# Loads of the second layer's expert blocks released by the gating of eight blocks before instead of by its landed results

## The chip, the cores and the metric

One core of a Trainium2 chip runs the whole kernel. The metric is the device time of one execution in microseconds (us), the median over several.

## What is computed

A two-layer vision transformer on 128 images. Each image is cut into 64 patches; with a class token it has 65 tokens of 128 numbers, 8320 tokens in all. Layer 0 has an attention and a mixture of 32 experts; layer 1 has a decay-weighted mixing within each image and a mixture of 16 experts with 512 hidden units, top 2 per token. The change touches this last part. Cut to what matters, the reference says:

```python
logits = xt @ router_w.T + router_b
probs = jax.nn.softmax(logits, axis=-1)
topk_p, topk_i = lax.top_k(probs, TOP_K)
gates = ...  # the two chosen probabilities of each token, 0 elsewhere
def expert_step(acc, packed):
    w1e, b1e, w2e, b2e, ge = packed
    h = jax.nn.gelu(xt @ w1e.T + b1e, approximate=False)
    y = h @ w2e.T + b2e
    return (acc + y * ge[:, None], None)
```

and the result is added to the layer's input, `h = h + ...`.

## The kernel before

**Dispatch.** Tokens go through in groups: 13 groups (`MG`) of 5 tiles of 128 tokens in the second layer. For each token and each of its two experts, GpSimd sends a row of 132 numbers to a list of that expert in DRAM, with an indirect DMA of 128 rows each (`send`, line 2554; ten sends for a group). A row holds the normalized token, and behind it where its result belongs (`PLACE`), its gate, and two numbers from which the token's own value is restored (`SPREAD`, `MEAN`). Tables made from the counts say which expert and which stretch of its list each block takes (`tb.entry`).

**Blocks.** The second layer's experts are worked off in 81 blocks (`L1.blocks`). 64 are full, with 256 list rows (two tiles); 17 are half, with 128 rows (one tile), every other block from 25 to 57. Block i uses buffers `u = i % 8`: `wblk` for an expert's weights (578 KB) and `xblk` for its rows (132 KB if full), both loaded by `load_part` from SyncE (lines 614 and 616), and `yblk` for the results. For each block:

- TensorE transposes the rows (`t1`, line 987, two blocks ahead), makes the first product (`t2`, line 1010 for full blocks, 1013 for half ones, one block ahead) and the second one (`t3`, line 1032).
- ScalarE copies the first weights to a rounded form (`high`) and applies GELU (line 1408).
- VectorE splits rows and weights for TensorE (`xT`, lines 2147 to 2152). Then `gated` restores the tokens' own values (line 2158), waits until `yblk` of eight blocks before has landed (line 2167), adds a bias to TensorE's second product (line 2173), and multiplies by the gate and adds (line 2184). The last of these instructions raises `y_ready`.
- GpSimd waits for `y_ready` and sends the results to their places in DRAM with one indirect DMA a tile (`send_results`, line 2582), which raise `y_out[u]` when they have landed. It reads the places out of `xblk`. In the first layer it reads them out of a buffer of their own, `place`, which VectorE fills (line 2169).

Because GpSimd reads `xblk` late, the loads of block i in the second layer wait at line 610 until the results of block i-8 have landed. In the first layer they wait for `y_ready`. Each engine does its work in the order in which it is written; SyncE's order is `sp_blocks`: the first eight blocks' loads, 17 writes of padding rows to the lists (`pads`), then one load a block. Before block 24 (`L1.early`) it waits until every list row and padding row has landed (`dispatched`).

**The last lists.** When the blocks begin, the ten sends of each of the last two groups are not all out: GpSimd sends 4 of group 11 ahead of the blocks and the other 16 one by one, one after each block's results.

**Finished groups.** A group whose results are complete is read back (`load_end`, line 725, 640 KB, four buffers), its two results a token are added by VectorE (`total`, line 2491) and stored by ScalarE's queue (line 1547). Groups 0 to 6 go among the blocks: SyncE reads them behind loads 65, 67, 69, 71, 73, 75 and 77 (`end_at`), VectorE adds them three blocks before those positions; their landings are implied by the waits of the loads. Groups 7 to 12 come after the blocks, with an explicit wait for landings (`landed`).

Of the kernel before, what the change touches and what calls it, by code (L numbers as in the profile page):

```python
# [23 lines left out]
U32 = mybir.dt.uint32  # L24
# [14 lines left out]
TILES = 5  # L39
ROWS = GT // TILES  # L40
HALF = GT // 2
TOP = 2
# [17 lines left out]
MG = TOKENS // (TILES * WIDE)  # L60
# [208 lines left out]
def build(nc, a, out):  # L269
    ctx = ExitStack()  # L270
    with ctx:
# [330 lines left out]
        def load_part(eng, l, u, j, part):  # L602

            k = K[l.name]
            i = l.unroll * j + u
            at, q, first, n = l.loads[i][part]
            entry = eng.value_load(tb.entry[0:1, at:at + 1], min_val=0, max_val=l.E * l.step - 1)  # L607
            e, r = entry // l.step, entry % l.step
            if l is L1:
                eng.wait_ge(k.y_out[u], k.y0[u] + 16 * l.packets(i))  # L610
            elif i >= l.unroll:
                eng.wait_ge(k.y_ready, i - l.unroll + 1)
            weights = third[u] if part == 2 else wblk_of[l.name][u][:, part * l.W:(part + 1) * l.W]
            eng.dma_start(weights, a[f"w_{l.name}"][bass.ds(e * 128, 128), :]).then_inc(k.blk_in[u], 16)  # L614
            tiles = max(n // 128, 1)
            eng.dma_start(xblk[u][first:first + n // tiles, q:q + tiles, :].rearrange("p q w -> p (q w)"),  # L616
                          lists[l.name][bass.ds(r, n), :].rearrange("(p q) w -> p (q w)", q=tiles))\
                .then_inc(k.blk_in[u], 16)
# [34 lines left out]
        @block.sync  # L653
        def _(sp):
            def load_patches(g, h, j):
                for c in range(CHUNKS):
                    sp.wait_ge(chunk_used[h][c], j)
                    sp.dma_start(xin[h][c][:, :, :].rearrange("p k n -> p (k n)"),
                                 a["x_main"][bass.ds(g * CHUNKS + c, 1), :, :].rearrange("o p n -> (o p) n"))\
                        .then_inc(chunk_in[h][c], 16)  # L660
                    if c == CHUNKS - 1:
                        sp.dma_start(xrest[h][:, :], a["x_rest"][bass.ds(g, 1), :, :]
                                     .rearrange("o p n -> (o p) n")).then_inc(chunk_in[h][c], 16)
            pairs(sp, load_patches)
            def load_rows(g):
                h, j = g % 2, g // 2
                if j > 0:
                    sp.wait_ge(m_free[h], j)
                sp_group_in(sp, "L0", g, h, yin, m_in[h])

            def load_distance(g):
                if g > 0:
                    sp.wait_ge(m_spread, g)
                sp.dma_start(m_dist[:, :, :].rearrange("p t c -> p (t c)"), a["distance"][g]).then_inc(dist_in, 16)

            def load_difference(g):
                h = g % 2
                if g > 1:
                    sp.wait_ge(delta_ps, 2 * (g - 1))
                sp.dma_start(m_delta[h][:, :, :].rearrange("p t c -> p (t c)"), a["difference"][g])\  # L680
                    .then_inc(delta_in[h], 16)

            def mid_class(g):

                done = (g + 1) * TILES * WIDE - 1
                return L0.class_of(done // (TILES * ROWS))

            def landed(l, enough):

                for b in range(max(0, enough - NB), enough):  # L690
                    sp.wait_ge(K[l.name].y_out[b % NB], K[l.name].y0[b % NB] + 16 * (l.packets(b) + l.tiles_of(b)))

            def rows_landed(g):
                landed(L0, L0.enough(mid_class(g)))
                load_rows(g)

            def early(g):
                if g + 2 >= 0:
                    yield 5, load_difference, g + 2
                yield 6, rows_landed, g + 3  # L700
                if g + 2 >= 0:
                    yield 7, load_distance, g + 2

            among = Among(early)
            for h in range(2):
                for c in range(CHUNKS):
                    sp.wait_ge(chunk_used[h][c], GROUPS // 2)
            sp_blocks(sp, L0, among)
            among.left()
            rows_landed(LAST + 4)  # L710
            load_difference(LAST + 3)
            load_distance(LAST + 3)
            load_difference(LAST + 4)
            rows_landed(LAST + 5)
            for g in range(LAST + 4, MG):
                if g + 2 < MG:
                    rows_landed(g + 2)
                if g + 1 < MG:
                    load_difference(g + 1)
                load_distance(g)  # L720

            def load_end(g, u, j):
                if j > 0:
                    sp.wait_ge(e_ready, g - NZ + 1)
                sp.dma_start(end_y[u].rearrange("p t k d -> p (t k d)"),
                             results["L1"].rearrange("(g p t k) d -> g p (t k d)", g=MG, p=WIDE, t=TILES)[g, :, :])\
                    .then_inc(e_in[u], 16)

            for u in range(NB):
                sp.wait_ge(K["L1"].y_out[u], K["L1"].y0[u])  # L730
            sp_blocks(sp, L1, ends(load_end, 0))

            def load_left(g, u, j):
                landed(L1, L1.enough(L1.class_of(g)))
                load_end(g, u, j)
            ends_left(load_left)


        @block.tensor
# [818 lines left out]
        def _(dve):  # L1558
# [563 lines left out]
            def expert_blocks(l, behind=None):  # L2122
# [39 lines left out]
                def gated(u, j):  # L2162
                    i = U * j + u
                    p2 = u % 2
                    restore(u, j)
                    Q = l.tiles_of(i)
                    dve.wait_ge(k.y_out[u], k.y0[u] + 16 * l.packets(i))
                    if l is L0:
                        dve.tensor_copy(place[:, u, :], xblk[u][:, :, PLACE].bitcast(U32))
                    dve.wait_ge(k.y_ps, k.i0 + i + 1)  # L2170
                    y = ps[:, banks(l, i)[2], 0:Q * D].rearrange("p (q d) -> p q d", q=Q)
                    if l.FC > 1:
                        dve.tensor_tensor(yblk[u][:, 0:Q, :], y,  # L2173
                                          wblk[u][:, None, l.W - D:l.W].to_broadcast([128, Q, D]), ALU.add)\
                            .then_inc(y_biased, 1)
                        dve.wait_ge(y_biased, i + 1)
                        y = yblk[u][:, :, :]
                    dve.wait_ge(restored, k.i0 + i + 1)
                    of = [(0, 128, q, q) for q in range(Q)]
                    if l.mixed[i]:  # L2180
                        of = [(0, 128, 0, 0), (0, 64, 1, 1), (64, 128, 1, 2)]
                        y = ps[:, banks(l, i)[2], 0:3 * D].rearrange("p (q d) -> p q d", q=3)
                    for first, end, q, product in of:
                        ins = dve.scalar_tensor_tensor(yblk[u][first:end, q, :], y[first:end, product, :],  # L2184
                                                       xblk[u][first:end, q, GATE:GATE + 1],
                                                       xblk[u][first:end, q, 0:D], ALU.mult, ALU.add)
                    ins.then_inc(k.y_ready, 1)
# [311 lines left out]
        def _(pool):  # L2499
# [75 lines left out]
            def expert_blocks(l, behind=None):  # L2575
                k = K[l.name]
                def send_results(u, j):
                    pool.wait_ge(k.y_ready, k.i0 + l.unroll * j + u + 1)
                    past(pool, pool_passed)
                    for q in range(l.tiles_of(l.unroll * j + u)):  # L2580
                        where = place[:, u, q:q + 1] if l is L0 else xblk[u][:, q, PLACE:PLACE + 1].bitcast(U32)
                        pool.indirect_dma_start(  # L2582
                            out=results[l.name], out_offset=bass.IndirectOffsetOnAxis(ap=where, axis=0),
                            in_=yblk[u][:, q, :], in_offset=None, bounds_check=last, oob_is_err=False)\
                            .then_inc(k.y_out[u], 16)
                    if behind:
                        behind(l.unroll * j + u)

                if l is L0:
                    rounds(pool, l, send_results)  # L2590
                    return
                of = list(itertools.product((MG - 2, MG - 1), range(TILES * TOP)))[4:]
                for i in range(l.blocks):
                    send_results(i % l.unroll, i // l.unroll)
                    for g, n in of[i:i + 1]:
# [10 lines left out]

            for g in range(LAST + 1, MG - 2):
                send(L1, g, g % 2)
            send(L1, MG - 2, MG % 2, 0, 4)
            expert_blocks(L1)  # L2610


# [64 lines left out]
```

## Time and profile before

| | |
|---|---|
| median of 3 runs | 1091.51 us (1088.7 to 1091.65) |
| the profiled execution | 1087.39 us, span 1085.7 us |
| TensorE busy | 914.5 us (84%) |
| VectorE busy | 847.8 us (78%) |
| GpSimd busy | 678.9 us (63%) |
| ScalarE busy | 503.9 us (46%) |
| DMA | 246.57 MB, mean 227 GB/s |

The span runs from the first to the last instruction of one profiled execution; its time is beside it, and the runs of the median were made apart from it. Shares are over the whole span, in which stages of different kinds follow each other: patches and first attention to about 430 us, first experts to about 660, second mixing to about 800, second experts to about 1066, and the last groups.

### The profile page before, as it was taken

The page shows a single profiled execution, that of the slowest core. Times are in us where ns is not written, and L with a number is a line of the kernel's source. Part 1 is how long each engine was busy: PE and PEld are TensorE (multiplying, and loading weights), DVE is VectorE, ACT ScalarE, POOL GpSimd, SP SyncE. Part 2 cuts the span into 40 slices and gives each one's busy share as a digit, 9 for nine tenths or more (in the row PEclk, how much of TensorE's full clock was granted, in tenths as well). Part 3 has the DMA queues.
Part 4 walks back from the last instruction along what each step waited for, and adds up shares of the span by engine and source line. Part 5 has one row for each costly group of instructions (what it writes and reads, how often), then busy time and mean ns, then how long its engine had stood idle before and what let it go on. Part 6 is the DMA issues. An engine that isn't in the chain of part 4 may idle for free.

```text
span 1085.7 us, 21714 instructions
## 1 busy us (share of the span) xinstructions
PE 914.5 (84%) x6064; PEld 772.5 (71%) x6064; DVE 847.8 (78%) x3318; ACT 503.9 (46%) x1342; POOL 678.9 (63%) x622
## 2 busy tenths in 40 slices
PE   6999999999999987476776877778569999999992
PEld 2577666677777666475665766677469989999992
DVE  1488889898888998666677899888667877778983
ACT  1355555555555442211112554777435655556561
POOL 1016666666676645677677767777777775545553
PEclk9999999999999997578887988877769999999996
DMA  9956566655566304577779973865188688889986
GB/s 371 353 206 217 202 217 222 222 201 201 201 206 211 123 21 116 152 209 206 210 219 310 293 259 120 265 228 169 59 302 263 231 253 277 275 279 301 356 325 235
DMA packets 118664, 246.57 MB, mean 227 GB/s; under 512 B 20914, under 2 KB 85936, under 8 KB 112400
## 3 DMA queue, kind: packets, MB, share of 16 engines
q1 hardware_dynamic: 77440, 191.26, 52.7%
q0 software_dynamic: 18592, 34.68, 9.4%
q10 hardware_dynamic: 22512, 19.25, 5.8%
q8 instruction: 48, 0.79, 0.3%
q14 instruction: 72, 0.59, 0.2%
HBM read 201.68 MB, written 45.43 MB: 228 GB/s over the span
## 4 chain that ended last, share of the span: by engine, by line
PE 39%; DVE 20%; issue 11%; DMA 11%; ACT 7%; SPq 6%; POOL 4%; ACTq 1%; DVEq 0%; POOLq 0%
PE ps L1032 6%; DMA xin<-lists_L 4%; PE ps L1010 4%; PE ps L762 4%; DMA results_L<-xin 3%; PE ps L1130 3%; POOL results_L L2582 3%; PE ps L829 3%; PE ps L1133 3%; PE ps L813 2%; SPq L614 2%; SPq L616 2%; PE ps L786 2%; SPq L607 2%; ACT x_hi L1211 2%
## 5 line engine op out<-in xcount | busy, mean ns | idle before, releaser
L2554 POOL DMA_INDIRECT lists_L<-rows,slots x230 | 263.4, 1145 | 153.3 <-issue 151.7
L2582 POOL DMA_INDIRECT results_L<-xin x145 | 146.2, 1008 | 96.3 <-DVE xin L2184 64.0
L2582 POOL DMA_INDIRECT results_L<-xin,place x146 | 144.1, 987 | 58.8 <-issue 39.3
L762 PE MATMUL ps<-xin,w_emb 128*128 128x512 f32 x292 | 137.7, 608 | 9.9 <-DMA w_emb<-in_w_main 8.3
L1032 PE MATMUL ps<-xin,QK 128*128 128x128 f32 x838 | 115.5, 289 | 2.6 <-DVE xin L2184 2.5
L1032 PEld LDWEIGHTS ps<-xin,QK 128*128 128x128 f32 x838 | 107.8, 204 | 4.5 <-issue 4.1
L2563 POOL TENSOR_TENSOR x_lo<-xin,x_hi 128x2048 fp32r<-128x2048 f32 x13 | 60.1, 4623 | 63.5 <-ACT x_hi L1219 63.1
L987 PE MATMUL ps<-ident,xin 128*128 128x128 f32 x291 | 66.3, 309 | 38.2 <-DMA xin<-lists_L 35.1
L1408 ACT ACTIVATE QK<-ps,xin 128x256 f32<-128x256 f32 x164 | 64.3, 475 | 70.9 <-PE ps L1010 70.9
L762 PEld LDWEIGHTS ps<-xin,w_emb 128*128 128x128 f32 x292 | 52.8, 194 | 58.9 <-issue 48.1
L2158 DVE TENSOR_SCALAR xin<-xin 128x128 f32<-128x128 f32 x291 | 92.7, 367 | 0.6
L1032 PE MATMUL ps<-xin,UH 128*128 128x128 f32 x648 | 89.2, 283 | 2.7 <-DVE xin L2184 2.7
L1238 ACT ACTIVATE h0T<-ps 128x256 f32<-128x256 f32 x73 | 27.9, 383 | 134.1 <-PE ps L987 90.2
L1032 PEld LDWEIGHTS ps<-xin,UH 128*128 128x128 f32 x648 | 81.7, 198 | 3.9 <-issue 3.8
L1010 PE MATMUL ps<-x_hi,x_lo 128*128 128x256 f32 x256 | 78.6, 307 | 0.7 <-DVE x_lo L2152 0.7
L1005 PE MATMUL ps<-h0T,xin 128*128 128x128 f32 (+1 forms) x326 | 60.3, 323 | 17.6 <-ACT h0T L1238 6.4
L1010 PE MATMUL ps<-x_lo,x_hi 128*128 128x256 f32 x256 | 73.1, 286 | 0.0
L1010 PE MATMUL ps<-x_hi 128*128 128x256 f32 x256 | 73.1, 286 | 0.0
L987 PEld LDWEIGHTS ps<-ident,xin 128*128 128x128 f32 x291 | 38.6, 157 | 47.4 <-DMA xin<-lists_L 43.0
L1408 ACT ACTIVATE UH<-ps,xin 128x256 f32<-128x256 f32 (+1 forms) x160 | 55.6, 430 | 32.8 <-PE ps L1010 29.1
L2173 DVE TENSOR_TENSOR xin<-ps,xin 128x256 f32<-128x256 f32 x81 | 32.2, 397 | 49.2 <-PE ps L1032 49.2
L1005 PEld LDWEIGHTS ps<-h0T,xin 128*128 128x128 f32 x326 | 54.0, 238 | 20.4 <-issue 11.6
(408 smaller groups left out, 2436.4 us busy)
## 6 DMA issues: line engine op xcount, KB each, us to landing
xin<-in_x_main SPq DMA_DIRECT2D x48, 1536.0 KB, 6.7
xin<-in_w_L SPq DMA_DIRECT2D x81, 578.0 KB
xin<-in_w_L SPq DMA_DIRECT2D x98, 128.0 KB
xin<-lists_L SPq DMA_DIRECT2D x64, 132.0 KB
xin<-in_w_L ACTq DMA_DIRECT2D x65, 128.0 KB
x_hi<-results_L SPq DMA_DIRECT2D x13, 640.0 KB, 6.3
xin<-in_difference SPq DMA_DIRECT2D x13, 640.0 KB
xin<-in_distance SPq DMA_DIRECT2D x13, 640.0 KB, 6.6
```

The costliest lines, as they stand in the source:

```text
L762: mm = pe.matmul(psE[h], w_emb[:, k, :], xin[h][c][:, n, :], start=(k == 0), stop=False, skip_group_check=True)
L829: mm = pe.matmul(pair[2][:, c:c + SEQ], V[h][:, i, :], Pr[h][:, i, :], start=True, stop=True)
L987: mm = pe.transpose(ps[:, banks(l, i)[0], q * 128:(q + 1) * 128], xblk[b][:, q, 0:D], ident[:, :])
L1005: mm = pe.matmul(bank_h(i, f)[:, of_part], w1, xTb[p2][:, of_part], start=True, stop=True)
L1010: mm = pe.matmul(bank_h(i, f)[:, 0:n_in], w[p2][:, cols_f], x[p2][:, 0:n_in], start=(n2 == 0), stop=(n2 == 2), skip_group_check=True)
L1032: mm = pe.matmul(o, hTb[p2][:, f, rows_in], w2[:, f * D:(f + 1) * D], start=(f == 0), stop=(f == l.FC - 1))
L1130: mm = pe.matmul(o, matrix[:, t, 0:WIDE], m_norm[g % 2][:, t, :], start=True, stop=alone, skip_group_check=True)
L1408: ins = act.activation(hTb[p2][:, f, 0:n_in], ps[:, 2 + 2 * p2 + f // 2, f % 2 * l.block:f % 2 * l.block + n_in], ACT.Gelu, bias=b1)
L2158: ins = dve.tensor_scalar(xblk[u][:, q, 0:D], xblk[u][:, q, 0:D], xblk[u][:, q, SPREAD:SPREAD + 1], xblk[u][:, q, MEAN:MEAN + 1], ALU.mult ...
L2554: pool.indirect_dma_start(out=lists[l.name], out_offset=bass.IndirectOffsetOnAxis(ap=slots_of(l, g, h)[:, t, k:k + 1], axis=0), in_=buf[:, ...
L2563: pool.tensor_tensor(x_lo0[:, :, :].rearrange("p k n -> p (k n)"), xin[h][0][:, 0:KS, :].rearrange("p k n -> p (k n)"), x_hi0[:, :, :].rea ...
L2582: pool.indirect_dma_start(out=results[l.name], out_offset=bass.IndirectOffsetOnAxis(ap=where, axis=0), in_=yblk[u][:, q, :], in_offset=Non ...
```

## The change

The loads of the second layer wait for `y_ready` of the block eight before, as those of the first do. So that `xblk` is free by then, VectorE copies the places to `place` in the second layer too, and GpSimd reads them there. Since a load no longer implies a landing, each read of a finished group among the blocks now waits for the landings it needs (`end_landed`), the same call as after the blocks. GpSimd sends 6 of group 11's lists ahead of the blocks instead of 4, and 14 among them instead of 16.

```diff
@@ load_part @@
-            if l is L1:
-                eng.wait_ge(k.y_out[u], k.y0[u] + 16 * l.packets(i))
-            elif i >= l.unroll:
-                eng.wait_ge(k.y_ready, i - l.unroll + 1)
+            if i >= l.unroll:
+                eng.wait_ge(k.y_ready, k.i0 + i - l.unroll + 1)
@@ block.sync @@
-            sp_blocks(sp, L1, ends(load_end, 0))
-
-            def load_left(g, u, j):
+            def end_landed(g, u, j):
                 landed(L1, L1.enough(L1.class_of(g)))
                 load_end(g, u, j)
-            ends_left(load_left)
+            sp_blocks(sp, L1, ends(end_landed, 0))
+            ends_left(end_landed)
@@ vector, gated @@
                     dve.wait_ge(k.y_out[u], k.y0[u] + 16 * l.packets(i))
-                    if l is L0:
-                        dve.tensor_copy(place[:, u, :], xblk[u][:, :, PLACE].bitcast(U32))
+                    dve.tensor_copy(place[:, u, :], xblk[u][:, :, PLACE].bitcast(U32))
@@ gpsimd @@
-                        where = place[:, u, q:q + 1] if l is L0 else xblk[u][:, q, PLACE:PLACE + 1].bitcast(U32)
                         pool.indirect_dma_start(
-                            out=results[l.name], out_offset=bass.IndirectOffsetOnAxis(ap=where, axis=0),
+                            out=results[l.name], out_offset=bass.IndirectOffsetOnAxis(ap=place[:, u, q:q + 1], axis=0),
...
-                of = list(itertools.product((MG - 2, MG - 1), range(TILES * TOP)))[4:]
+                of = list(itertools.product((MG - 2, MG - 1), range(TILES * TOP)))[6:]
...
-            send(L1, MG - 2, MG % 2, 0, 4)
+            send(L1, MG - 2, MG % 2, 0, 6)
```

## Rows read from the trace of the kernel before

**Rows 1.** Windows over the block stage and its last part, with their columns' heading.
```profile
core 0: us, PE busy (x) PEld busy (x) DVE busy (x) ACT busy (x) POOL busy (x), PEclk, DMA share, GB/s
806.00:1066.00 260.00, 252.59 (x2181) 249.20 (x2179) 203.88 (x577) 150.37 (x381) 159.47 (x160) 1.00 0.86 285
1020.00:1050.00 30.00, 29.25 (x256) 29.06 (x255) 26.95 (x72) 18.12 (x44) 16.90 (x17) 1.00 1.01 377
```

**Rows 2.** Waits from 806 to 1066 us: total, times, longest, in us.
```profile
SPq L614 <- DMA results_L<-xin: 92.7, 49, 4.6
...
DVE xin L2173 <- PE ps L1032: 48.8, 70, 1.7
...
PE ps L987 <- DMA xin<-lists_L: 7.0, 11, 1.9
```

**Rows 3.** Chain that ended last, in order of time: start, us, what.
```profile
868.04 4.41 DMA results_L<-xin
...
873.21 5.14 DMA xin<-lists_L
```

**Rows 4.** Timeline of TensorE: transposes of blocks 8, 22, 46 and 72.
```profile
825.89 0.44 PE L987 MATMUL ps<-ident,xin 128*128 128x128 f32 x2 [0.77 <-DMA xin<-lists_L]
...
878.40 0.44 PE L987 MATMUL ps<-ident,xin 128*128 128x128 f32 x2 [1.91 <-DMA xin<-lists_L]
...
948.38 0.44 PE L987 MATMUL ps<-ident,xin 128*128 128x128 f32 x2 [1.03 <-DMA xin<-lists_L]
...
1029.62 0.44 PE L987 MATMUL ps<-ident,xin 128*128 128x128 f32 x2 [0.75 <-DMA xin<-lists_L]
```

**Rows 5.** Timeline of SyncE: pad rows, then the weight loads of these blocks.
```profile
806.48 13.47 SPq L591 DMA_DIRECT2D lists_L<-padrows  x16
820.91 0.35 SPq L614 DMA_DIRECT2D xin<-in_w_L  x1
...
872.65 0.33 SPq L614 DMA_DIRECT2D xin<-in_w_L  x1
...
942.01 0.33 SPq L614 DMA_DIRECT2D xin<-in_w_L  x1
...
1020.74 0.33 SPq L614 DMA_DIRECT2D xin<-in_w_L  x1
```

**Rows 6.** Timeline of VectorE: gating of blocks 14, 38 and 64.
```profile
857.60 0.61 DVE L2184 SCALAR_TENSOR_TENSOR xin<-xin 128x128 f32<-128x128 f32 x2
...
934.31 0.62 DVE L2184 SCALAR_TENSOR_TENSOR xin<-xin 128x128 f32<-128x128 f32 x2
...
1012.25 0.61 DVE L2184 SCALAR_TENSOR_TENSOR xin<-xin 128x128 f32<-128x128 f32 x2
```

**Rows 7.** VectorE: copies' durations (min/median/max) and group mean; then its timeline.
```profile
L2169 DVE COPY place<-xin x73: 148/164/428, 455.7 to 661.2; 128x2 uint32<-128x2 uint32 x73
...
L2169 DVE COPY place<-xin 128x2 uint32<-128x2 uint32 x73 | 14.6, 199 | 0.0
...
1020.39 0.42 DVE L2147 CAST x_hi<-ps 128x256 fp32r<-128x256 f32 x1
...
1025.54 0.42 DVE L2173 TENSOR_TENSOR xin<-ps,xin 128x256 f32<-128x256 f32 x1 [0.47 <-PE ps L1032]
...
1026.53 0.82 DVE L2491 TENSOR_TENSOR xin<-x_hi 128x640 f32<-128x640 f32 x1
1027.27 0.42 DVE L2147 CAST x_hi<-ps 128x256 fp32r<-128x256 f32 x1
```

**Rows 8.** Timeline of GpSimd: last send ahead, first results, lists after blocks 13, 15.
```profile
806.49 0.97 POOL L2554 DMA_INDIRECT lists_L<-values,slots  x1 [0.30 <-issue]
809.94 0.99 POOL L2582 DMA_INDIRECT results_L<-xin  x1 [2.49 <-DVE xin L2184]
...
865.46 0.97 POOL L2554 DMA_INDIRECT lists_L<-rows,slots  x1 [0.30 <-issue]
...
873.26 0.97 POOL L2554 DMA_INDIRECT lists_L<-rows,slots  x1 [0.30 <-issue]
```

## The prediction

> **What bounds the kernel now.** I read the page first, to find the stage that the diff touches: the second layer's expert blocks, 81 of them, run from about 806 to 1066 us of the span. Then the table of windows for that stage. TensorE is busy for 252.6 of its 260 us, at a granted clock of 1.00 (its 2.4 GHz level); VectorE for 203.9, GpSimd for 159.5, the DMA engines for 0.86 of the time [rows 1]. So the stage is TensorE's. Whatever the change does to the loads, it can't give more than TensorE's idle 7.4 us there.
>
> Next the waits of the stage. Nearly all of TensorE's idle time has one reason: 7.0 us in 11 pieces, each before the transposes that open a block (line 987), each ended by a load that arrives [rows 2]. The SyncE queue, which issues these loads, waits 92.7 us in 49 pieces at line 614 for landed results [rows 2]. The chain of waits joins the two. A result leaves GpSimd at 868.04 and lands 4.41 us later; that frees block 22's load, which takes 5.14 us; and TensorE starts the block at 878.40, 1.91 us late [rows 3, 4]. What the diff removes is therefore on the path, but only where the load comes late. Elsewhere it is hidden.
>
> **Waits removed.** Today load i needs block i-8's results in DRAM; afterwards it needs only VectorE's last gating instruction of block i-8 (line 2184). For three of the late blocks I compare the time at which TensorE wanted the block (its start less the idle time) with both releases.
> - Block 22: wanted at 878.40 - 1.91 = 876.5, issued at 872.65, so 3.8 us of lead where 5.75 were needed. Gating of block 14 ended at 857.60 + 0.61 = 858.2: lead 18.3 us [rows 4 to 6].
> - Block 46: wanted at 947.35, issued at 942.01, lead 5.3, needed 6.4. Gating of block 38 ended at 934.93: lead 12.4 [rows 4 to 6].
> - Block 72: wanted at 1028.87, issued at 1020.74, lead 8.1, needed 8.9. Gating of block 64 ended at 1012.86: lead 16.0 [rows 4 to 6].
>
> The slowest of these loads took 8.9 us, and the shortest new lead is 12.4. So these waits go entirely. The 0.77 us before block 8 stay: its load left at 820.91 because the queue had been issuing the 16 pad rows since 806.48 (13.47 us), which the diff leaves where they are [rows 4, 5]. Gain: 7.01 - 0.77 = 6.24 us. What is late next? Nothing on TensorE's side: in these 260 us its only releaser by name is the load.
>
> **The copy of the places.** VectorE now does the copy of line 2169 for these 81 blocks too. The first layer runs it 73 times at a mean of 199 ns [rows 7], so 81 x 0.2 = 16 us of VectorE. It stands between restoring the rows and the wait for TensorE's product. Over the stage VectorE waits there for TensorE 48.8 us in 70 pieces [rows 2]: that hides it. The tightest stretch is where the additions of finished groups (line 2491) run among full blocks: two blocks and one addition take from 1020.39 to 1027.27, 6.88 us, of which VectorE idles 0.47 [rows 7]. Two copies take 0.40 of that. TensorE's period there is the same 6.88, so the copy still fits, by 0.07 us a pair, and costs nothing. If it did not fit it would cost at most 2 x 0.428 - 0.47 = 0.39 us a pair with the longest copy seen [rows 7], and 0 with the mean one; over the 7 additions 0 to 2.7 us. I take 0, as the mean is the nearer row, and keep 2.7 for the range.
>
> **Two lists in front.** GpSimd idles 2.49 us before the first results at 809.94. A list send follows every 1.27 us (0.97 and 0.30 of issue), so two more after 806.49 end at 810.3, and the first results leave 0.36 us later [rows 8]. Nothing on TensorE's path waits for them any more. In return the last list leaves after block 13's results, where a list starts at 865.46 today, instead of after block 15's, at 873.26 [rows 8]. SyncE waits for all lists before load 24. With the 4.41 us that a scatter took to land [rows 3], they are down at 865.8 + 4.4 = 870.2 instead of 877.7. That is 7.5 us earlier, while the blocks have by then moved up by less than the whole gain, 6.2 us. With 877.7 no idle piece fell on block 24, so with 870.2 none will. Cost 0; GpSimd would have to fall at least 1.3 us behind today's pace before anything could show.
>
> **The reads of finished groups.** Their loads (line 725) now wait for landings themselves. Only the first, at block 65, can hold the queue: it waits for block 57's results, which is what load 65 waits for today, so it is no later than now. Load 66, behind it, may lose a landing's 4.4 us of a lead like block 72's 16. Cost 0. VectorE's own wait before it reuses a result buffer (line 2167) is for results eight blocks old, 8 x 3.44 = 27.5 us in full blocks; block 14's, in the worst of GpSimd's backlog, were down at 872.45, 14.2 us after their gating at 858.2 [rows 3, 6]. Cost 0. The end (results of the last block, four reads of finished groups, addition, store) only moves up.
>
> **The sum.** The profiled execution took 1087.39 us (span 1085.7). 1087.39 - 6.24 + 0 = 1081.2. The three timed runs lie higher, with a median of 1091.51, so 4.12 above the execution whose rows I used. The same gain from that median gives 1091.51 - 6.24 = 1085.3, my forecast.
>
> **Rivals.**
> - *Loads that take longer (0.14).* The engines are busy for 0.86 of the stage and 1.01 in 1020 to 1050, at 377 GB/s [rows 1]. Loads issued 7 to 14 us earlier lie beside each other in the queues and each may take longer. For it: the slowest of the three rows took 8.9 us in that very stretch. Against it: the bytes are the same, and a load must take over 12 us before TensorE notices. With half of the waits left: 1091.5 - 3.1 = 1088.4.
> - *The queue is held all the same (0.08).* SyncE goes in order, so if the lists before load 24 or the landing at block 65 hold it, the loads behind are as late as today. This is the change that doesn't do what it says. It takes GpSimd to fall behind by 1.3 us or more, or a landing at block 65 far over 4.4 us; the send rows show an even pace of 1.27 us. Time: 1090 to 1091.5.
> - *VectorE becomes the bound (0.05), the slower side.* If the copy waits for GpSimd's sends, it isn't 0.2 us long. The first layer's longest is 0.428 against a shortest of 0.148 [rows 7]; a send lasts 0.97 [rows 8]. The addition takes 1027.27 - 1026.53 = 0.74 us of VectorE's time, so a full block without it takes (6.88 - 0.47 - 0.74)/2 = 2.83 of a period of 3.44 and has room for 0.61 [rows 7]; beside an addition there is room for 0.235. Copies of 0.75 us would cost 14 x (0.75 - 0.235) = 7.2 us in the last third and 50 x (0.75 - 0.61) = 7.0 over the other full blocks, 14.2 in all, less the 6.24 gained: 1091.5 + 8.0 = 1099.5. From about 0.63 us a copy the change loses. Of 73 copies none reaches that. The Trainium skill has a rule that leads there: SBUF — State Buffer, "Who interferes with whom", says that VectorE copies in a two-port mode and GpSimd share a port pair under an exclusive lock, and that the later one blocks fully. By that rule alone a copy could last a whole send more. The rows of the first layer, where the sends run as well, agree at most for a part of one.
>
> The rest, 0.03, is unforeseen. The forecast has 0.70.
>
> **How the numbers follow.** Under the forecast alone I expect 1083 to 1087.5: the gain of 6.24, up to 2.7 back for the copy, and about as much to the other side for an execution with more late loads than the profiled one. The range of 1081.5 to 1089.5 adds the rival of longer loads and runs that differ by 3 us among themselves. It leaves out the held queue, the slow copies and the tails. A measurement of this kernel tells about 0.3%, 3.3 us, from no change. Faster by more: nearly all of the forecast (0.69) and a third of the longer loads (0.05), so 0.74. Within: the rest of those and the held queue, 0.21. Slower: 0.05.
>
> **What would show it.** In the profile after: TensorE idle for loads in the stage about 0.8 us, at block 8; line 614's wait at SyncE released by line 2184 instead of a DMA; the copy in the stage at about 0.2 us x81, VectorE's busy time there up by 16 us and its idle time down by as much; the first results about 0.4 us later; the chain of waits through the blocks all TensorE. The prediction is wrong if pieces of idle time before line 987 stay in the second half of the stage, if TensorE waits at lines 1010 or 1032 for VectorE, or if its busy time in the stage rises.

## The result, and the profile after

The changed kernel takes 1083.08 us, the median of 6 runs (1082.49 to 1085.35); the kernel before, in 6 runs beside them, 1090.11 (1087.42 to 1091.93). The ratio is 0.9943, with a 95% interval of 0.9926 to 0.996: 6.2 us faster by the ratio, 7.0 by the two medians. The forecast was 1085.3 in a range of 1081.5 to 1089.5, and faster had 0.74. The sign, the place and the range were right. The sum was not right in its parts: one term was too small, one was missing, and the two partly cancel.

The profiled execution of the changed kernel has a span of 1081.3 us, against 1085.7. Windows over its block stage and the last part, columns as in [rows 1]:

```profile
806.00:1066.00 260.00, 252.68 (x2198) 252.24 (x2197) 211.69 (x664) 150.68 (x386) 164.44 (x164) 0.99 0.87 291
1020.00:1050.00 30.00, 30.00 (x264) 30.00 (x263) 28.16 (x84) 17.86 (x44) 17.38 (x18) 1.00 0.78 287
```

The first window now holds all of the stage from 806 us on and some of what follows it, because the stage ends at 1059 us. So its sum for TensorE is about that of [rows 1], and that says nothing. The second window lies inside the stage in both: TensorE went from 29.25 to 30.00 of 30 us.

Waits from 806 to 1066 us (total, times, longest): SyncE for its loads, VectorE for the second product, and TensorE for a load, first in the queue of weight loads (PEld) and then in that of matmuls (PE).

```profile
SPq L612 <- DVE xin L2180: 66.4, 55, 1.9
...
DVE xin L2169 <- PE ps L1029: 33.3, 54, 1.6
...
PEld ps L984 <- DMA xin<-lists_L: 0.8, 1, 0.8
...
PE ps L984 <- DMA xin<-lists_L: 0.6, 1, 0.6
```

Line 612 is the old 614, and line 2180 the gating of the old 2184. SyncE still waits at line 612 for a long time, but for the gating and no longer for a landing, and that wait is idle time of an engine off the path. Of TensorE's 11 pieces [rows 2] one is left, before block 8 (old line 987 is 984). The reason is where it was, 16 pad rows ahead of load 8 in SyncE's queue; SyncE's timeline and TensorE's:

```profile
809.01 14.12 SPq L591 DMA_DIRECT2D lists_L<-padrows  x16
824.24 0.35 SPq L612 DMA_DIRECT2D xin<-in_w_L  x1
```

```profile
829.37 0.44 PE L984 MATMUL ps<-ident,xin 128*128 128x128 f32 x2 [0.63 <-DMA xin<-lists_L]
```

The end of the stage on GpSimd, the results of blocks 78, 79 and 80 (two sends each). This is what the forecast did not have:

```profile
1056.07 0.98 POOL L2577 DMA_INDIRECT results_L<-xin,place  x1 [1.16 <-DVE xin L2180]
1057.35 0.98 POOL L2577 DMA_INDIRECT results_L<-xin,place  x1 [0.30 <-issue]
1061.71 1.04 POOL L2577 DMA_INDIRECT results_L<-xin,place  x1 [3.38 <-issue]
...
1065.61 0.98 POOL L2577 DMA_INDIRECT results_L<-xin,place  x1 [0.30 <-issue]
```

Gating of block 79 ended at 1058.5, yet its first send starts at 1061.71, after 3.38 us in which GpSimd waits for nothing that the profile shows. In the kernel before no such gap stands there; its first send of block 79 follows the gating:

```profile
1065.96 0.98 POOL L2582 DMA_INDIRECT results_L<-xin  x1 [0.96 <-DVE xin L2184]
1067.24 1.44 POOL L2582 DMA_INDIRECT results_L<-xin  x1 [0.30 <-DVE xin L2184]
...
1070.27 0.98 POOL L2582 DMA_INDIRECT results_L<-xin  x1 [0.30 <-issue]
```

The chain that ended last runs through TensorE alone from block 8 to the end of the blocks, then through that send and the read behind it:

```profile
824.83 4.50 DMA xin<-lists_L
...
1055.60 3.72 PE ps L1029 x32
...
1065.61 2.26 DMA results_L<-xin,place
...
1069.85 7.87 DMA w_emb<-results_L
```

**The balance of the two profiles.** Take as the stage the time from block 2's transposes, the first inside it, to the end of the last matmul. Block 2's rows, before and after:

```profile
803.36 0.63 PE L987 MATMUL ps<-ident,xin 128*128 128x128 f32 x2
```

```profile
806.82 0.63 PE L984 MATMUL ps<-ident,xin 128*128 128x128 f32 x2
```

- The stage took 1065.9 - 803.4 = 262.5 us before and 1059.3 - 806.8 = 252.5 after: 10.0 less (10.06 in hundredths).
- It began 3.46 us later (806.82 - 803.36). The two lists can't have made that: in all five profiles with six lists in front the two added ones are sent 3 us or more after block 2's start (here at 809.95 and 811.22). In the profiles of this study block 2 starts between 800.0 and 806.0 with four lists in front (eight kernels) and between 803.6 and 807.8 with six (five kernels). I take it as spread between executions; what makes it stays open.
- The tail, from the last matmul to the end of the span, took 1085.7 - 1065.9 = 19.8 us before and 1081.3 - 1059.3 = 22.0 after: 2.2 more.

-10.06 + 3.46 + 2.20 = -4.40, the difference of the spans.

### The profile page after: what moved, and what is told of

The parts are those of the page before. It is cut to its first block, busy times and chain, and to the rows that moved or that the text cites. A ratio compares the mean times of both kernels' runs of the same rounds, so it can differ in the third digit from the quotient of the medians.

```text
span 1081.3 us, 21742 instructions
## 1 busy us (share of the span) xinstructions
PE 911.6 (84%) x6064; PEld 772.7 (71%) x6064; DVE 852.0 (79%) x3399; ACT 501.8 (46%) x1342; POOL 677.5 (63%) x622
## 4 chain that ended last, share of the span: by engine, by line
PE 46%; DVE 17%; issue 11%; SPq 8%; POOL 6%; ACT 5%; DMA 5%; ACTq 1%; DVEq 0%; POOLq 0%
PE ps L1029 12%; PE ps L1007 8%; POOL lists_L L2550 5%; PE ps L759 4%; PE ps L826 3%; PE ps L810 2%; SPq L614 2%; SPq L612 2%; SPq L607 2%; ACT x_hi L1208 2%; PE ps L984 2%; PE ps L1127 2%; PE ps L798 2%; PE ps L752 2%; PE ps L1130 1%
## 5 line engine op out<-in xcount | busy, mean ns | idle before, releaser
L2577 POOL DMA_INDIRECT results_L<-xin,place x291 | 289.6, 995 | 152.5 <-DVE xin L2180 79.5
L1002 PEld LDWEIGHTS ps<-h0T,xin 128*128 128x128 f32 x326 | 53.4, 236 | 21.4 <-issue 10.7
L1235 ACT ACTIVATE atok<-ps 104x640 f32<-104x640 f32 x16 | 11.3, 705 | 104.0 <-PE ps L776 104.0
```

Source lines behind the costliest of these rows:

```text
L1002: mm = pe.matmul(bank_h(i, f)[:, of_part], w1, xTb[p2][:, of_part], start=True, stop=True)
L1235: return act.activation(dst, src, ACT.Copy)
L2577: pool.indirect_dma_start(out=results[l.name], out_offset=bass.IndirectOffsetOnAxis(ap=place[:, u, q:q + 1], axis=0), in_=yblk[u][:, q, :] ...
```

## The experiments

Below, "stage", "tail" and "idle" (TensorE's, for loads, by the matmul rows) are meant as above. Ratios are to the kernel before, on the same chip.

**The changed kernel again (e1)**, with no edit, as the yardstick for the runs beside it.

> The changed kernel once more, as the base of the others. My theory: the whole gain is TensorE's waits for late loads in the second layer's blocks, so 0.992 to 0.996 of the kernel before (5 to 8 us less), with the stage about 10 us shorter by its first and last matmuls and TensorE idle for loads under 1 us. Rival (part of the difference came from where this one execution happened to stand before and after the stage): another ratio, 0.997 or more, with the same stage.

Measured: 1083.08 us, ratio 0.9946 (0.9926 to 0.9967). Stage 252.6, tail 21.9, and the same 3.38 us before block 79's results. So the gap belongs to the kernel, not to one execution.

**Only four lists in front (e2).** The change without its last part.

```diff
-                of = list(itertools.product((MG - 2, MG - 1), range(TILES * TOP)))[6:]
+                of = list(itertools.product((MG - 2, MG - 1), range(TILES * TOP)))[4:]
...
-            send(L1, MG - 2, MG % 2, 0, 6)
+            send(L1, MG - 2, MG % 2, 0, 4)
```

> The changed kernel with 4 lists in front instead of 6. My theory: the lists are off TensorE's path, so the same as the changed kernel within 1 us; the last list leaves GpSimd some 8 us later (about 878 instead of 870 us of the span) and SyncE's wait before load 24 grows from 5.3 to about 13 us, with the lead of load 24 still above 4 us. Rival: the lists in front carry part of the gain by keeping SyncE's wait before load 24 short; then TensorE idles before blocks 24 to 28 and 2 us or more of the gain go.

Measured: 1078.85 us, 0.991 (0.9893 to 0.9926), 4.2 us below e1, which ran beside it. Stage 252.8 as before, idle 0.7 in two pieces, tail 20.1. The results of block 79 leave on time:

```profile
1058.33 0.98 POOL L2577 DMA_INDIRECT results_L<-xin,place  x1 [0.96 <-DVE xin L2180]
```

So the lists in front seem to cost time instead of nothing. The tail shows 1.8 of the 4.2 us. Block 2 starts 2.2 us earlier than in e1 (805.56 against 807.81), ahead of the two added sends in e1 (811.37 and 812.65), so that part isn't theirs. The intervals of the two ratios meet at 0.9926, so the size of the difference is less sure than the gap itself.

**Only the copy (e3).** The kernel before, with the copy and GpSimd's reads out of `place` in both layers, and its loads still waiting for landings.

```diff
-                    if l is L0:
-                        dve.tensor_copy(place[:, u, :], xblk[u][:, :, PLACE].bitcast(U32))
+                    dve.tensor_copy(place[:, u, :], xblk[u][:, :, PLACE].bitcast(U32))
...
```

> The kernel before with the places copied by VectorE and read from their own buffer in both layers; loads still wait for landed results. My theory: the copy hides behind VectorE's waits for TensorE, so the same as before within 1.5 us. Rival (the copy costs): it delays the gating, and with it the results and the loads that wait for them, by 0.2 us a block where VectorE has no room, 1 to 3 us slower.

Measured: 1088.6 us, 1.0008 (0.9994 to 1.0023). The stage is 260.7 us, with 6.3 us of idle in nine pieces. The copy costs nothing that shows.

**Only the lists (e4).** The kernel before with six lists in front.

```diff
-            send(L1, MG - 2, MG % 2, 0, 4)
+            send(L1, MG - 2, MG % 2, 0, 6)
```

> The kernel before with 6 lists in front instead of 4 and nothing else. My theory: the loads up to 22 depend on results that have the same 14 lists ahead of them as before, so block 22's wait of 1.9 us stays; at most 1 us faster from later loads. Rival (GpSimd's backlog is the true cause and two sends less relieve it): 2 to 3 us faster, block 22's wait gone.

Measured: 1090.57 us, 1.0009 (0.9988 to 1.003). The stage is 262.6 us, so no gain; the gap stands before block 79's results here too, and the tail is 22.6. The tail is 2.8 us longer than in the kernel before; by the ratio the whole kernel is 1.0 us slower, and the interval would allow 2.8.

```profile
1070.05 1.04 POOL L2582 DMA_INDIRECT results_L<-xin  x1 [3.38 <-issue]
```

e3 and e4 together leave the gain to the one part that remains: what releases the loads. e2 has that part without the added lists and has the whole gain.

**How late may a load be (e5, e6, e9)?** On the version with four lists, the loads of the second layer wait for a block one, two or three later.

```diff
-                eng.wait_ge(k.y_ready, k.i0 + i - l.unroll + 1)
+                eng.wait_ge(k.y_ready, k.i0 + i - l.unroll + 1 + (1 if l is L1 else 0))
```

(2 and 3 in e6 and e9.)

> The changed kernel with 4 lists in front, and its second layer's loads released one block later (gating of block i-7). The lead of a load shrinks by one block, 2 to 3.4 us: for block 46 from 11.8 to about 9. My theory (a load needs 4 to 9 us, all earlier release is spare): the same as the run with the 4 lists, within 1 us, and TensorE idle for loads under 1.5 us. Rival (earlier is better without limit, because the DMA engines are then fed evenly): 2 to 4 us of the gain go.

Measured: 1080.45 us, 0.993 (0.9904 to 0.9955), with one wait of 1.74 us, at block 24.

> The same with the loads released two blocks later (gating of block i-6): lead of block 46 about 6.4 us, of full blocks about 9. My theory: now the slow loads come late again in the stretch of half blocks, where a load took 6.4 us and more in the kernel before; TensorE idles 1 to 5 us for loads, so 1 to 6 us slower than with the 4 lists. Rival (loads take 5 us once nothing else holds them): no change.

Measured: 1079.65 us, 0.9927 (0.99 to 0.9953), with one wait of 1.61 us, at block 8. Nothing in the rest of the stage, though the loads have 3.4 us less again in full blocks (8.8 us of lead, after 12.2 in e5). Load 46 on SyncE, and its block's transposes on TensorE, which follow 6.3 us later without a wait:

```profile
935.74 0.33 SPq L612 DMA_DIRECT2D xin<-in_w_L  x1
...
942.00 0.38 PE L984 MATMUL ps<-ident,xin 128*128 128x128 f32 x2
```

> The changed kernel with 4 lists in front and the second layer's loads released three blocks later (gating of block i-5): lead about 4 us in the half blocks, 5.5 in full ones, which is where the kernel before had it (3.8 to 8.1). My theory, after two blocks later cost nothing: between 4 and 6 us of lead it turns, so TensorE idles again before many blocks, 5 to 20 us, and most or all of the gain is gone (ratio to before 0.998 to 1.01). Rival (the waits of the kernel before came from something other than short leads, such as traffic of the results): few waits, ratio under 0.995.

Measured: 1107.86 us, 1.0175 (1.0142 to 1.0208). One block more, and about 27 us are lost (0.0248 of 1089 us by the two ratios): the stage is 278.6 us, TensorE waits 18 times for loads in it, 17 of them up to 1066 us, and load 46 leaves 4.7 us ahead of its transposes (949.37 and 954.08).

```profile
PE ps L984 <- DMA xin<-lists_L: 20.1, 17, 2.9
```

My reading, which no run separates, is that it feeds itself: a late load makes the block late, and the block's gating releases later loads late. The cliff lies between two and three blocks, and not at one figure of lead. In e9 blocks 11 to 17 wait for nothing with 5.4 us of lead, while blocks 68, 72 and 76, in the part where the finished groups are read, wait 2.93, 2.04 and 2.70 us, and their loads had left 8.2, 7.4 and 8.1 us before their transposes. In e6 those three had 8.8 us and no wait. So how much lead a load needs differs within the stage.

**Three copies (e7).** Two more copies a block into a buffer that nobody reads.

```diff
                     dve.tensor_copy(place[:, u, :], xblk[u][:, :, PLACE].bitcast(U32))
+                    if l is L1:
+                        for n_ in range(2):
+                            dve.tensor_copy(extra_places[:, u, n_, :], xblk[u][:, :, PLACE].bitcast(U32))
...
```

> The changed kernel with 4 lists in front and two more copies of the places a block, to a buffer that nobody reads: three copies, 0.6 us a block. By the room I worked out (0.235 us a block beside an addition, 0.61 elsewhere): 14 x (0.6 - 0.235) = 5 us slower than with the 4 lists, all of it from block 62 on, TensorE idle until VectorE there. Rival (VectorE works two blocks ahead of TensorE's need and carries a shortage over): under 1.5 us slower.

Measured: 1079.25 us, 0.9922 (0.9896 to 0.9949), against 0.991 in e2 and 0.9927 in e6: not slower by anything that the intervals show, where 5 us were expected. The stage is 254.1, of which 2.14 are block 8's wait. From 1000 to 1050 TensorE (first column) never idles, with VectorE (third) at 48.08 of 50:

```profile
1000.00:1050.00 50.00, 50.00 (x438) 50.00 (x437) 48.08 (x169) 29.93 (x72) 29.34 (x30) 1.00 0.81 304
```

VectorE's timeline says why three copies fit where I had room for one:

```profile
1007.37 0.17 DVE L2166 COPY place<-xin 128x2 uint32<-128x2 uint32 x1
1007.44 0.24 DVE L2169 COPY extra_places<-xin 128x2 uint32<-128x2 uint32 x2
...
1007.77 0.42 DVE L2173 TENSOR_TENSOR xin<-ps,xin 128x256 f32<-128x256 f32 x1
```

The second copy starts 0.07 us after the first, which is shown as 0.17 long. The rows overlap: a copy's row is the time that it takes, and the engine is free for the next one earlier.

**Pads out of the way of load 8 (e8).** On the version with four lists, the 16 pad rows go in four parts behind loads 10 to 13.

```diff
-            pads(sp, l, 0, PADS[l.name])
+            if l is L0:
+                pads(sp, l, 0, PADS[l.name])
...
+                i = l.unroll * j + u
+                if l is L1 and NB + 2 <= i < NB + 6:
+                    pads(sp, l, 4 * (i - NB - 2), 4 * (i - NB - 1))
```

> The changed kernel with 4 lists in front, and SyncE's pad rows sent in four parts behind the loads of blocks 10 to 13 instead of ahead of block 8's load, so that load 8 goes out as soon as block 0 is gated. My theory: the last 0.7 us of idle time before block 8 go and the loads behind have lead to spare, so 0.7 us faster than with the 4 lists. Rival (the pads hold loads 11 to 14 instead): no gain, an idle piece at block 12 to 15.

Measured: 1080.37 us, 0.9928 (0.9902 to 0.9954). Block 8's wait is gone, as it should be if the pads were its cause. But 2.11 us came back at block 24:

```profile
879.55 0.44 PE L988 MATMUL ps<-ident,xin 128*128 128x128 f32 x2 [2.11 <-DMA xin<-lists_L]
```

Load 24 left at 874.82, held until the last list had landed. In the changed kernel it leaves at 872.50 and has a lead of 11.9 us; in e2 it leaves at 878.83 with 4.6. So the lists in front do buy something, an earlier load 24. With four of them block 24 is at the edge once the blocks run faster: its load leaves 4.6 us ahead of its transposes in e2 and e6, without a wait; here and in e5 it leaves 4.7 and 5.2 us ahead, and of these 2.11 and 1.74 are the wait. With six lists and the new release none of the profiles has a wait there.

**The gap on GpSimd (e10, e11).** Where GpSimd stands still for over 1.5 us without a reason that the profile shows, counted in sends of results from the end: with four lists in front at the 52nd and 30th, with six at the 52nd, 34th and 4th (in e4 also at the 105th). One theory: it comes at fixed places of the instruction stream. e10 shifts the stream of the changed kernel by eight instructions on GpSimd.

```diff
             send(L1, MG - 2, MG % 2, 0, 6)
+            for _ in range(8):
+                past(pool, pool_passed)
```

> The changed kernel as it is, 6 lists in front, with eight semaphore increments more on GpSimd right before its blocks; they take under 0.5 us in all. In every profile with 6 lists GpSimd stands still for 3.4 us before the results of block 79, in none with 4. Theory A (the stall sits at fixed places of GpSimd's instruction stream): it moves some 8 instructions towards the start, to about block 77, where it is hidden, and the kernel gets 2.4 us faster than the changed one (ratio to before 0.992). Theory B (it belongs to the number of lists or to what is in flight then): it stays at block 79, and so does the time.

Measured: 1080.58 us, with the gap where it was and as long, so the theory of fixed places fell. The ratio is 0.9921 (0.9896 to 0.9946), 0.0022 below the changed kernel's own, and the intervals overlap widely. The profile shows the same tail (21.9) and gap, and a stage of 254.1 us, 1.6 longer, of which 1.4 are a longer wait at block 8 (2.06 us against 0.63). Nothing in it is faster, so I take the 0.0022 as spread.

```profile
1063.23 1.04 POOL L2577 DMA_INDIRECT results_L<-xin,place  x1 [3.38 <-issue]
```

e11 sends five lists ahead (`[5:]`, `send(L1, MG - 2, MG % 2, 0, 5)`).

> The changed kernel with 5 lists in front. Theory A: the order of two sends changes the stream before block 14 alone, and the stall sits somewhere else than with 4 or 6, by a place or two; if it is off block 79 the tail is 20 us instead of 22. Theory B (two more sends in front as such cause it): a stall of half the size, or one at block 79 as with 6.

Measured: 1079.63 us, 0.9909 (0.988 to 0.9938). The gap is at block 80's first send now, 1.63 us, and the tail is 21.4:

```profile
1058.39 1.44 POOL L2577 DMA_INDIRECT results_L<-xin,place  x1 [0.30 <-DVE xin L2180]
...
1061.46 0.98 POOL L2577 DMA_INDIRECT results_L<-xin,place  x1 [1.63 <-issue]
```

It was at the 4th send from the end with six lists, is at the 2nd with five, and with four there is none so late; the one before it is at the 34th, 32nd and 30th. So these two places move by one block for each list that goes in front, and the one at the 52nd stays. They depend on the order of the sends, and not on how many went before, which is the same at block 79 in all of them. What makes the gap is not settled. In its last 1.7 us (1060.00 to 1061.71 in the changed kernel) the DMA engines move nothing, so a transfer under way isn't what GpSimd waits for, and no packet of the instruction queues falls into it in any of the five profiles with six lists.

One rival is left. The send that ends the gap starts just before the end of two additions of VectorE, both operands of which lie in the buffers:

```profile
1060.34 0.82 DVE L2487 TENSOR_TENSOR xin<-x_hi 128x640 f32<-128x640 f32 x1
1061.08 0.82 DVE L2487 TENSOR_TENSOR xin<-w_emb 128x640 f32<-128x640 f32 x1
```

The send is 0.18 to 0.19 us ahead of that end in all five profiles with six lists (here 1061.71 and 1061.90), while e11's gap, beside which VectorE does nothing, is 1.63 us and not 3.38. So a part of the 3.38 us may be a wait for these additions. No run moves them, and they can't be the whole cause, since the same additions make no such gap in e2.

**Six lists and spread pads (e12),** with the eight increments of e10.

```diff
-            pads(sp, l, 0, PADS[l.name])
+            if l is L0:
+                pads(sp, l, 0, PADS[l.name])
...
             send(L1, MG - 2, MG % 2, 0, 6)
+            for _ in range(8):
+                past(pool, pool_passed)
```

> The changed kernel, 6 lists in front, with the pad rows spread behind loads 10 to 13 and the eight increments on GpSimd. If block 8's wait (0.7), block 24's (0 to 2 with 4 lists, none with 6) and the stall of the tail (2.4) are separate, all three are gone: TensorE idle under 0.3 us in the stage, tail 20 us, ratio to before 0.989 to 0.992, at least as fast as the run with the 4 lists. Rival (spread pads keep the lists' condition before load 24 late, or the stall stays): no faster than the changed kernel, 0.994.

Measured: 1079.83 us, 0.9902 (0.9876 to 0.9928). The stage is 252.4 us. One wait of 0.56 us is left, at block 14, and load 24 has its 11.9 us again; the gap of 3.38 us stays, and the tail is 22.7.

e2, e11 and e12 lie clearly below the kernel before (0.991, 0.9909, 0.9902) and by their medians below the changed one (0.9943 and 0.9946, and 0.9921 as e10). The lead over the changed kernel is 1 to 4 us; e12's interval, to 0.9928, overlaps the change's from 0.9926 by a hair, e11's by more. Which of the three is best these runs do not say. The plainest is e2: the change with the lists left as they were.

## Why the prediction was right, and where it wasn't

- **The waits removed: right, and mis-sized.** All pieces but block 8's are gone, SyncE's release is the gating, and e3 and e4 show that neither other part gives anything alone. The term "7.01 - 0.77 = 6.24 us" was too small: the stage is 10.0 us shorter. I had read the idle time from the matmul rows, whose ends are modelled and overlap what follows. The row of the weight loads in the kernel before, which I did not read, has more pieces and more time:

```profile
PEld ps L987 <- DMA xin<-lists_L: 10.3, 16, 2.1
```

  It went to 0.8, a gain of 9.5, near the 10.0 measured. The other runs bear this reading out. The stage less the waits of the weight loads in it is 251.3 to 252.4 us in thirteen of the fourteen profiles, e3 and e4 among them (254.0 in e9); less the waits of the matmul rows it goes from 251.7 to 255.5 in these thirteen, and the three with many waits stand at the top. My cap, "it can't give more than TensorE's idle 7.4 us", rested on the same rows and was wrong in the same way.
- **The copy: cost 0 was right, its working was not.** I priced it at 0.2 us of VectorE and left room for 0.07 us a pair. Its row is about that long,

```profile
L2165 DVE COPY place<-xin x81: 154/160/431, 810.6 to 1058.9; 128x2 uint32<-128x2 uint32 x81
```

  but it takes only about 0.07 us of the engine (e7), and VectorE's busy time from 806 to 1066 us rose by 7.8 us, not by 16. A pair of blocks with an addition is still 6.88 us, with 0.38 of idle time where there were 0.47 [rows 7]: 0.09 for two copies.

```profile
1012.96 0.42 DVE L2169 TENSOR_TENSOR xin<-ps,xin 128x256 f32<-128x256 f32 x1 [0.39 <-PE ps L1029]
...
1016.47 0.15 DVE L2165 COPY place<-xin 128x2 uint32<-128x2 uint32 x1
1016.54 0.41 DVE L2169 TENSOR_TENSOR xin<-ps,xin 128x256 f32<-128x256 f32 x1
...
1019.84 0.42 DVE L2169 TENSOR_TENSOR xin<-ps,xin 128x256 f32<-128x256 f32 x1 [0.38 <-PE ps L1029]
```

  So the rival of a bound VectorE was further off than its numbers said. The rule of the Trainium skill beside it (SBUF — State Buffer, "Who interferes with whom": the later one of a VectorE copy in a two-port mode and GpSimd blocks fully) would allow copies longer by a whole send. The longest of the 81, with a send under way for more than half of the stage, is 0.431 us against a send's 0.98, and the 162 extra ones of e7 reach 0.448. These rows do not show a block for a whole send, as the first layer's did not. They do show one for the end of a send, which I had overlooked. The longest copy, and the send under way beside it:

```profile
831.08 0.98 POOL L2577 DMA_INDIRECT results_L<-xin,place  x1 [0.30 <-issue]
...
831.63 0.43 DVE L2165 COPY place<-xin 128x2 uint32<-128x2 uint32 x1
```

  Both end at 832.06. The 17 copies that begin 0.55 to 0.68 us into a send take 0.25 to 0.43 us, and each ends within 0.04 us of its send; the 18 that begin earlier in a send take 0.15 to 0.16. So the trace agrees with the rule for the last 0.4 us or so of a send, and what a copy can lose by it is about 0.3 us.
- **Two lists in front: the step that failed.** I had "Cost 0", with the first results 0.36 us later. They are not later: they leave 0.8 us after their gating in both kernels. The cost is at the other end, where I wrote that the end "only moves up": the gap of 3.38 us before block 79's results, a tail 2.2 us longer, and by e1 and e2 4.2 us in the median. How much of that is the lists' is not shown: e10 and e12 send six ahead too, have the gap and a long tail, and their ratios are 0.9921 and 0.9902 against e2's 0.991. What the profiles show of the lists is the 1.8 to 2.8 us of the tail. I had looked at what the moved sends pass (the first results, load 24) and not at the sends behind them. What I said of load 24, that no idle piece would fall on it, came true; I did not see that with four lists one would (e5, e8).
- **The reads of finished groups: the cost of 0 was right, "only the first" was not.** The wait for a landing at block 65 makes load 66 late by 2.8 us (it leaves at 989.38, gating of block 58 ended at 986.54), and its lead of 13.1 us covers that. The read behind load 75 holds the queue as well: load 76 leaves at 1023.31, 2.4 us after the gating of block 68, with a lead of 13.5.

```profile
988.22 0.33 SPq L723 DMA_DIRECT2D w_emb<-results_L  x1
989.38 0.33 SPq L612 DMA_DIRECT2D xin<-in_w_L  x1
```

- **The other rivals.** Loads that take longer: not borne out for this change, since TensorE has no wait in the late part, and e6 runs there on 8.8 us of lead. I had said that a load must take over 12 us before TensorE notices; from block 12 on the shortest lead came out at 11.6, in the half blocks. The queue held all the same: three places, load 24 (4.0 us behind the gating of block 16, for the lists), load 66 (2.8) and load 76 (2.4), and no loss.
- **The sum.** I subtracted 6.24 from the median and got 1085.3. With the stage and the tail as the profiles show them it would have been 1091.5 - 10.0 + 2.2 = 1083.7, and 1083.08 was measured; the later start of the stage, 3.5 us, is left out here as spread. The two errors, 3.8 us of gain and 2.2 us of cost that were missing, have opposite signs, which is why the forecast came within 2.2 us. That is luck, and so is a part of the last agreement: from the 1090.11 of six runs the same sum gives 1082.3, and the two profiled executions differ by 4.3 us where the medians differ by 7.0.

## What to carry to other kernels

Let a load wait for the last reader of its buffer, and copy out the few numbers that a slow reader still needs. Read an engine's idle time from every row that names it, the weight loads' too, before it is used as a cap on a gain. A lead has a cliff: loads released two blocks later cost nothing that shows, three blocks later about 27 us, so ask how far a tuned lead stands from it. And an edit to the order of a queue off the path is checked at its end, where nothing hides it.

## What the runs showed of the hardware

- GpSimd stood still for 1.6 to 3.4 us before some indirect sends for no reason in the profile (up to 4.0 in e9). The late places moved with the order of the sends, one block a list, and not with eight more instructions (e1, e2, e4, e10, e11). Its cause stays open.
- Small copies behind each other on VectorE start 0.07 us apart while the first is shown as 0.17 (e7). Counting rows by their length overstates such work more than twofold.
- GpSimd's sends and VectorE's work lengthen each other. A copy of 128x2 that begins 0.55 to 0.68 us into a send of 0.98 ends with the send (17 copies of the changed kernel, 0.25 to 0.43 us instead of 0.16). All nine sends of its stage that took over 1.2 us (up to 1.44) began while VectorE worked on a subtraction with both operands in the buffers (line 2147, the old 2150).
- Waits by the weight loads' rows account for the length of the stage to within 1.1 us in thirteen profiles, those by the matmul rows to within 3.8.
